# A three-part transformer kernel: gathers set between scatters, four places for normalised rows, and ScalarE in place of VectorE for attention's normalisation

## The chip, the cores and the metric

The kernel runs on 1 core of one Trainium2 chip. The metric is the device time of one execution in microseconds (us), as the median of several runs. The profile comes from one further execution of the same program. A measurement of this kernel tells about 0.5% from no change.

## The reference, cut to what matters

The input x has 4096 rows (2 sequences of 2048) of D = 256 floats. Three layers follow one another, each on a layer norm of x, each added to x:

```
x = x + 0.5 * ffn(layernorm(x))       # "FFN", first time
x = x + attention_and_moe(layernorm(x))
x = x + 0.5 * ffn(layernorm(x))       # "FFN", second time

ffn(h):   scores = sigmoid(h @ gate_w.T)              # 16 experts
          ids = top 512 rows of each expert           # "expert choice"
          eo = (silu(h[ids] @ gw.T + gb) * (h[ids] @ up.T + ub)) @ down.T + db
          out[ids] += eo * score;  out += shared_ffn(h)   # hidden 512

attention_and_moe(x):                                  # heads 16, width 16, chunks of 64
          y = rmsnorm(x) ; q, k = phi(rope(y @ Wq + bq)), phi(rope(y @ Wk + bk))
          v, g = y @ Wv + bv, sigmoid(y @ Wg + bg)
          S, Z run along the chunks of the sequence:   # linear attention
             S += k.T v ; Z += sum k ; o = g * (q S) / (q Z + 1e-6)
          x = x + o @ Wo + bo
          top 2 of 8 experts for each row, at most 1280 rows an expert:
          out[tok] += gate * (gelu(rmsnorm(x)[tok] @ W1 + b1) @ W2 + b2)
```

All products are wanted in float32. The kernel splits both factors of a large product in a high and a low part and takes three products of these (high by high, low by high, high by low).

## The kernel before, in words

Rows are kept in 32 tiles of 128. There are seven stretches in order of time, and the tensors' names tell them apart: f1s (front of the first FFN, `ffn_front`), f1e (its experts, `run_experts`), ma (`attention`), mr (routing), m (lists of the Mixture's rows), me (the Mixture's experts, `run_experts` again), f2s and f2e (second FFN). Each stretch is a block: every engine has its own queue of instructions there, written out in the order in which they are issued, with semaphores between the engines, and the next block begins when all engines are through.

**The front of the FFN.** Eight groups of four tiles. For each, VectorE takes means and variances, GpSimd (`root`) makes `rstd` and `shift`, ScalarE's `norm(g)` writes the normalised rows into `h[:, g % 2]`, a buffer with two places; TensorE's `turn(g)` transposes them, ScalarE casts the high part and `store(g)` sends the rows to DRAM (`h_rows`), where the gathers will read them. `norm(g)` therefore waits for the store of group g - 2 (`h_out`) and for its transposes (`turn_done`). Then come the products of the shared FFN in `STEPS` = 32 steps with their down products two steps behind, and between them the search for each expert's top 512 rows, whose lists are made by one-hot products: `slots(half, part)` is 32 products of 64 columns on TensorE, `place_ids(half)` 16 small operations of VectorE that turn the result into row numbers. `slots(1, 0)` and `slots(1, 1)` stand behind the last down product and `place_ids(1)` behind the last `add_shared`, which adds the shared FFN's output to x in `out`, another buffer with two places, which SyncE's queue (SP) stores.

**First rows.** At the end of a front and of the lists, `gather_first` on GpSimd fetches the first expert's rows: one indirect DMA for each tile of 128 rows (4 tiles for the FFN, 10 for the Mixture), and the block ends when they have been issued. `ids.shape[2]` is that number of tiles.

**The experts.** `run_experts` does E experts (16 for the FFN, called gated, with NT = 4 tiles; 8 for the Mixture, with NT = 10). The Mixture's hidden layer is 8 slices of 128 by C = 3 groups of up to 4 tiles, so S = 24 stages for an expert. In stage st TensorE makes the input product `into(e, st)` and the down product of two stages before, `down(e, st - 2)`; between them ScalarE takes the gelu (L1036) and VectorE splits it in a high and a low part. The rows of expert e + 1 are transposed in stages 13, 15, 17, 19 and 21 (`ITEM_AT`), two tiles each time, out of `rows`, a buffer with NT places. The output leaves PSUM by ScalarE (`read_sums`) and VectorE (`add_bias`, which counts `out_done`), and GpSimd scatters it tile by tile, adding in DRAM. `read_sums` of expert e + 1's last stages waits for `landed`, which GpSimd counts when the scatters of expert e - 1 are through.

GpSimd's queue in the experts is: the gathers of expert 1; then for each expert e, `gather_after(e + 1)`, which waits until the rows of expert e + 1 have been transposed and then issues all NT gathers of expert e + 2 in one go (L928), and then the NT scatters of expert e (L949), each behind its `out_done`. The gathers of expert e + 2 and the scatters of expert e so stand at the end of expert e and in the first stages of expert e + 1.

**Attention.** 32 tiles, two sequences by turns. `pipelined` gives each engine a list of steps with lags: in round r the engine does each step of its list for tile r - lag, in the order of the list. Ten rounds fill the pipeline, 22 run in a loop (11 times two), ten drain it. The steps that matter here are `stat` (VectorE, lag 0, last in its list: L1459 and L1461), `root` (GpSimd, lag 0, last, five operations), `norm` (VectorE, lag 1: two operations, L1466 and L1469, the layer norm into `x2_all` and the row scaled once more into `a`), TensorE's transposes of `a`, `split_at` (ScalarE, lag 2, first in its list, high part, L1405) and `split_low` (VectorE, lag 2, L1474). VectorE's list is:

```
pipelined(dve, T, [(10, add_out), (4, add_bias), (2, split_low), (6, state0), (7, state1), (5, feature),
                   (1, norm), (8, divide), (0, stat)])
```

and ScalarE's is `split_at` (2), `exp_rot` (5), `half_tanh` (4), `copy_qt` (6), `values` (5), `copy_ot` (9), `sum_squares` (10). SP loads tile r + 2's row of `x_all` (L1255) once `a` of a tile is done.

## Time and profile before

| | |
|---|---|
| runs | 2588.79, 2579.51, 2581.09 us; median 2581.09 |
| profiled execution | 2590.76 us, of which the span of the trace is 2589.0; mean granted TensorE clock 0.927 |
| busy, TensorE (PE) | 2288.6 us, 88% of the span |
| busy, VectorE (DVE) | 1764.9 us, 68% |
| busy, GpSimd (POOL) | 912.0 us, 35% |
| busy, ScalarE (ACT) | 846.1 us, 33% |

The stretches of the span, in us: front of the first FFN to about 229, its experts to 800, attention 820 to 1112, routing to 1162, lists to 1234, the Mixture's experts to 1777, front of the second FFN 1784 to 2011, its experts to 2583. In the profile PE is TensorE's matmuls and PEld its weight loads, which overlap; L12 is line 12 of the kernel before; a DMA share is the mean busy share of 16 DMA engines; the clock is the share of full speed (2.4 GHz) that the throttle granted. The idle time in brackets behind an instruction is that of its engine just ahead of it, with the event that came last before it ended.

### The profile page before, as it was taken

What the parts mean: (1) busy time and instruction counts of PE and PEld (TensorE: products, weight loads), DVE (VectorE), ACT (ScalarE), POOL (GpSimd) and SP (SyncE); (2) the same over time, 40 slices, a digit from 0 to 9 for tenths busy, and PEclk for the clock granted to TensorE, in tenths of its full rate; (3) what the DMA queues carried; (4) which work ended last, traced back from release to release, by engine and by line L of the source; (5) the groups of instructions that cost most, each with busy time, mean ns of one, the idle gap of its engine ahead of it and who ended that gap; (6) DMA issues with size and microseconds to landing.
All of it is one profiled execution on the core that took longest, in us unless ns stands there. A gap on an engine that the chain in (4) does not pass through costs nothing. (4 is left out here: it accounts for less than half of the span.)

```text
span 2589.0 us, 38567 instructions
## 1 busy us (share of the span) xinstructions
PE 2288.6 (88%) x13308; PEld 1974.0 (76%) x13308; DVE 1764.9 (68%) x3725; ACT 846.1 (33%) x1542; POOL 912.0 (35%) x965
## 2 busy tenths in 40 slices
PE   6998999999994888873799999993899899999997
PEld 5787888888883666661688888892778788888886
DVE  4785777777773999854465656553576777777775
ACT  5221333333331333310233333332321333333332
POOL 4201333333323877621144444424320233333332
PEclk9998999999997898955899999996999899999998
DMA  5003444444432000031243344325102344444442
GB/s 166 25 25 111 110 127 136 135 121 131 130 95 57 25 28 29 28 97 43 66 81 75 77 76 80 77 29 149 46 25 66 108 123 136 136 122 129 130 126 45
DMA packets 154183, 227.99 MB, mean 88 GB/s; under 512 B 33312, under 2 KB 104736, under 8 KB 153888
## 3 DMA queue, kind: packets, MB, share of 16 engines
q1 hardware_dynamic: 103184, 157.82, 19.5%
q0 software_dynamic: 39936, 55.93, 12.2%
q10 hardware_dynamic: 10896, 12.07, 1.4%
q8 instruction: 99, 1.62, 0.2%
q14 instruction: 68, 0.56, 0.1%
HBM read 171.36 MB, written 54.39 MB: 87 GB/s over the span
## 5 line engine op out<-in xcount | busy, mean ns | idle before, releaser
L1036 ACT ACTIVATE me_act_f<-me_in,me_bias 128x512 f32<-128x512 f32 (+1 forms) x192 | 118.6, 620 | 324.3 <-PE me_in L125 276.6
L123 PE MATMUL f1e_in<-f1e_xt_hi,f1e_w_hi 128*128 128x512 f32 x512 | 203.5, 398 | 2.4 <-DVE f1e_xt_lo L1096 2.4
L123 PE MATMUL f2e_in<-f2e_xt_hi,f2e_w_hi 128*128 128x512 f32 x512 | 203.4, 397 | 2.4 <-DVE f2e_xt_lo L1096 2.4
L125 PE MATMUL f2e_in<-f2e_xt_hi,f2e_w_lo 128*128 128x512 f32 x512 | 202.8, 396 | 0.0
L125 PE MATMUL f1e_in<-f1e_xt_hi,f1e_w_lo 128*128 128x512 f32 x512 | 202.7, 396 | 0.0
L124 PE MATMUL f1e_in<-f1e_xt_lo,f1e_w_hi 128*128 128x512 f32 x512 | 202.3, 395 | 0.0
L124 PE MATMUL f2e_in<-f2e_xt_lo,f2e_w_hi 128*128 128x512 f32 x512 | 202.2, 395 | 0.0
L1036 ACT ACTIVATE f1e_silu<-f1e_in,f1e_bias 128x512 f32<-128x512 f32 x128 | 88.2, 689 | 340.5 <-PE f1e_in L125 290.2
L1036 ACT ACTIVATE f2e_silu<-f2e_in,f2e_bias 128x512 f32<-128x512 f32 x128 | 88.2, 689 | 340.3 <-PE f2e_in L125 290.2
L1125 DVE CAST me_act_hi<-me_act_f 128x512 fp32r<-128x512 f32 (+1 forms) x192 | 74.6, 389 | 178.1 <-ACT me_act_f L1036 156.0
L123 PE MATMUL me_down<-me_w_hi,me_act_hi 128*128 128x256 f32 x640 | 184.2, 288 | 0.3 <-issue 0.2
L124 PE MATMUL me_down<-me_w_lo,me_act_hi 128*128 128x256 f32 x640 | 181.1, 283 | 0.3 <-issue 0.3
L125 PE MATMUL me_down<-me_w_hi,me_act_lo 128*128 128x256 f32 x640 | 180.5, 282 | 0.3 <-issue 0.3
L123 PE MATMUL me_in<-me_xt_hi,me_w_hi 128*128 128x512 f32 (+1 forms) x384 | 141.1, 368 | 35.8 <-DVE me_act_lo L1126 20.9
L1122 DVE SCALAR_TENSOR_TENSOR f1e_act_f<-f1e_in,f1e_bias,f1e_silu 128x512 f32<-128x512 f32 x128 | 96.0, 750 | 112.5 <-ACT f1e_silu L1036 85.5
L1122 DVE SCALAR_TENSOR_TENSOR f2e_act_f<-f2e_in,f2e_bias,f2e_silu 128x512 f32<-128x512 f32 x128 | 96.0, 750 | 112.4 <-ACT f2e_silu L1036 84.1
L949 POOL DMA_INDIRECT out<-f2e_out,f2e_sid x64 | 107.6, 1682 | 167.1 <-DVE f2e_out L1139 152.4
L949 POOL DMA_INDIRECT after_ffn<-f1e_out,f1e_sid x64 | 107.3, 1677 | 166.8 <-DVE f1e_out L1139 152.2
L949 POOL DMA_INDIRECT after_moe<-me_out,me_sid x80 | 131.5, 1643 | 92.7 <-DVE me_out L1139 70.0
L123 PE MATMUL f1e_down<-f1e_w_hi,f1e_act_hi 128*128 128x256 f32 x512 | 147.3, 288 | 0.0
L123 PE MATMUL f2e_down<-f2e_w_hi,f2e_act_hi 128*128 128x256 f32 x512 | 147.2, 288 | 0.0
L125 PE MATMUL f2e_down<-f2e_w_hi,f2e_act_lo 128*128 128x256 f32 x512 | 144.3, 282 | 0.0
(429 smaller groups left out, 7053.7 us busy)
## 6 DMA issues: line engine op xcount, KB each, us to landing
f_raw<-in_ffn_w SPq DMA_DIRECT2D x256, 384.0 KB
m_raw<-in_moe_w SPq DMA_DIRECT2D x64, 256.0 KB
f1s_x_all<-in_x SPq DMA_DIRECT2D x8, 512.0 KB, 8.5
f_h<-f1s_h ACTq DMA_DIRECT2D x8, 512.0 KB, 3.0
after_ffn<-f1s_out SPq DMA_DIRECT2D x8, 512.0 KB, 3.1
ma_x_all<-after_ffn SPq DMA_DIRECT2D x32, 128.0 KB
after_moe<-ma_x_all SPq DMA_DIRECT2D x32, 128.0 KB
m_h<-mr_h SPq DMA_DIRECT2D x16, 256.0 KB, 2.2
```

What stands on the lines that cost most here:

```text
L123: pe.matmul(out, lh, rh, start=first, stop=False, skip_group_check=True)
L124: pe.matmul(out, lh, rl, start=False, stop=False, skip_group_check=True)
L125: return pe.matmul(out, ll, rh, start=False, stop=last, skip_group_check=True)
L949: pool.indirect_dma_start(out=acc, out_offset=bass.IndirectOffsetOnAxis(ap=sid[:, j:j + 1], axis=0), in_=out[:, b, j, :], in_offset=None, ...
L1036: act.activation(dst[:, st % 2, 0:n], ps_in[st % 2][0][:, 0:n], func, bias=bias[:, b, f:f + 1]).then_inc(silu_done, 1)
L1122: own.step(dve.scalar_tensor_tensor(act_n, ps_in[st % 2][1][:, 0:n], bias[:, b, F_T + f:F_T + f + 1], silu[:, st % 2, 0:n], ALU.add, ALU.m ...
L1125: own.step(dve.tensor_copy(hi_n, act_n))
```

## The change

Three sets of edits.

First, in the experts. `gather_first` fetches `FIRST_TILES` = 4 tiles; where NT is larger (the Mixture), the other six are gathered at the start of `run_experts`. For the Mixture, each of expert 1's ten gathers waits for one further down product, and those of expert e + 2 are issued one behind each scatter of expert e. The FFN keeps its order. Second, in the front. Normalised rows have `H_RING` = 4 places (the two of `h` and, while it isn't used, the two of `out`), so that `norm(g)` waits for group g - 4; the first two `add_shared` wait for the stores and transposes of those places. `slots(1, 0)` and `slots(1, 1)` move ahead of the last two down products, `place_ids(0)` goes from the start of step `STEPS` to its end, and `place_ids(1)` moves ahead of the last `add_shared`. Third, in attention. ScalarE takes `norm` over, first in its list, as two activations with a scale and a shift; GpSimd's `root` has three operations instead of five (one power over two columns, one shift) and VectorE's `stat` also waits for `a_done` ahead of L1461.

```diff
...
@@ -48,7 +48,7 @@
...
-RAW_RING = 4
+RAW_RING, FIRST_TILES = 4, 4
...
@@ -156,7 +156,7 @@
 
     pool.tensor_copy(first.gid[:], ids[:, 0, :]).then_inc(first.gid_done, 1)
     wait_apart(pool, first.gid_done, 1)
-    for j in range(ids.shape[2]):
+    for j in range(FIRST_TILES):
         pool.indirect_dma_start(out=first.rows[:, j, :], out_offset=None, in_=h_rows,
                                 in_offset=bass.IndirectOffsetOnAxis(ap=first.gid[:, j:j + 1], axis=0)
                                 ).then_inc(first.rows_in[j // 2], 16)
...
+    H_RING = 4
...
+        h_ring = [h[:, 0], h[:, 1], out[:, 0], out[:, 1]]
...
@@ -331,7 +333,7 @@
                 for k in range(K):
                     for t in range(GT):
                         ins = pe.transpose(turned[g % 2][:, k * GC + t * P:k * GC + (t + 1) * P],
-                                           h[:, g % 2, t, k * P:(k + 1) * P], ident[:])
+                                           h_ring[g % H_RING][:, t, k * P:(k + 1) * P], ident[:])
                 ins.then_inc(turn_done, 1)
...
+            last = {STEPS: lambda: slots(1, 0), STEPS + 1: lambda: slots(1, 1)}
             extra = {LISTS + 1: [lambda: offset(0)], LISTS + 2: [lambda: offset(1)], LISTS + 3: [turn_positions],
                      LISTS + 9: [lambda: slots(0, 0)], LISTS + 10: [lambda: slots(0, 1)]}
             for g in range(G + 1):
@@ -438,10 +441,10 @@
                     into(n)
                 for one in extra.get(n, ()):
                     one()
+                if n in last:
+                    last[n]()
                 if n >= LAG:
                     down(n - LAG)
-            slots(1, 0)
-            slots(1, 1)
...
             def norm(g):
-                u = g % 2
+                u = g % H_RING
                 act.wait_ge(x_in_s[g], 16)
                 act.wait_ge(rstd_done, g + 1)
-                if g >= 2:
-                    act.wait_ge(h_out[u], 16 * (g // 2))
-                    act.wait_ge(turn_done, g - 1)
+                if g >= H_RING:
+                    act.wait_ge(h_out[u], 16 * (g // H_RING))
+                    act.wait_ge(turn_done, g - H_RING + 1)
                 for t in range(GT):
-                    ins = act.activation(h[:, u, t], x_all[:, g * GT + t], ACT.Identity, bias=shift[:, g, t:t + 1],
+                    ins = act.activation(h_ring[u][:, t], x_all[:, g * GT + t], ACT.Identity, bias=shift[:, g, t:t + 1],
                                          scale=rstd[:, g, t:t + 1])
                 ins.then_inc(h_done, 1)
...
             def store(g):
                 act.wait_ge(h_done, g + 1)
-                act.dma_start(rows_of(h_rows, g), h[:, g % 2]).then_inc(h_out[g % 2], 16)
+                act.dma_start(rows_of(h_rows, g), h_ring[g % H_RING]).then_inc(h_out[g % H_RING], 16)
...
         def _(dve):
@@ -575,6 +578,9 @@
                 dve.wait_ge(down_done, (g + 1) * F_T)
                 if g >= 2:
                     dve.wait_ge(out_stored[g % 2], 16 * (g // 2))
+                else:
+                    dve.wait_ge(h_out[2 + g], 16 * (G // H_RING))
+                    dve.wait_ge(turn_done, G)
                 for t in range(0, GT, 2):
                     ins = dve.scalar_tensor_tensor(out[:, g % 2, t:t + 2], ps_down[:, t:t + 2, :], 0.5,
                                                    x_all[:, g * GT + t:g * GT + t + 2, :], ALU.mult, ALU.add)
...
-            lists = {STEPS: lambda: place_ids(0), LISTS: choose, LISTS + 1: add_ties, LISTS + 2: place, LISTS + 3: split_positions}
+            lists = {LISTS: choose, LISTS + 1: add_ties, LISTS + 2: place, LISTS + 3: split_positions}
...
@@ -678,9 +684,12 @@
                     activate(n)
                 if n - 1 >= LISTS and n - 1 < STEPS:
                     activation_low(n - 1)
+                if n == STEPS:
+                    place_ids(0)
+                if n + 1 == STEPS + LAG:
+                    place_ids(1)
                 if ends_group(n + 1):
                     add_shared((n + 1 - LAG) // F_T - 1)
-            place_ids(1)
             dve.wait_ge(ids_done, 2)
...
-            def gather(e):
-                own.step(pool.tensor_copy(gid[:], gather_ids[:, ds(e, 1), :].rearrange("p e j -> p (e j)")), apart=True)
-                for j in range(NT):
-                    pool.indirect_dma_start(out=rows[:, j, :], out_offset=None, in_=h_rows,
-                                            in_offset=bass.IndirectOffsetOnAxis(ap=gid[:, j:j + 1], axis=0)
-                                            ).then_inc(rows_in[j // 2], 16)
-
-            def gather_after(e):
+            def take_ids(dst, ids, e):
+                own.step(pool.tensor_copy(dst[:], ids[:, ds(e, 1), :].rearrange("p e j -> p (e j)")), apart=True)
+
+            def gather_tile(j):
+                pool.indirect_dma_start(out=rows[:, j, :], out_offset=None, in_=h_rows,
+                                        in_offset=bass.IndirectOffsetOnAxis(ap=gid[:, j:j + 1], axis=0)
+                                        ).then_inc(rows_in[j // 2], 16)
+
+            def rows_free(e):
 
                 pool.wait_ge(gates_set, e + 1)
                 pool.wait_ge(turned, e * NI + NI)
                 for i in range(NI):
                     wait_apart(pool, rows_in[i], e * 32 + 32)
-                gather(e + 1)
-
-            gather_after(0)
+
+            def scatter_tile(e, b, j):
+                pool.wait_ge(out_done, (e + OUT0) * NT + j + 1)
+                pool.indirect_dma_start(out=acc, out_offset=bass.IndirectOffsetOnAxis(ap=sid[:, j:j + 1], axis=0),
+                                        in_=out[:, b, j, :], in_offset=None, compute_op=ALU.add
+                                        ).then_inc(scattered, 16)
+
+            if NT > FIRST_TILES:
+                take_ids(gid, gather_ids, 0)
+                for j in range(FIRST_TILES, NT):
+                    gather_tile(j)
+            rows_free(0)
+            take_ids(gid, gather_ids, 1)
+            for j in range(NT):
+                if not gated:
+                    pool.wait_ge(down_done, DOWN0 + j + 2)
+                gather_tile(j)
 
             def one(e, b, left):
+
                 if left > 1:
-                    gather_after(e + 1)
-
-                own.step(pool.tensor_copy(sid[:], scatter_ids[:, ds(e, 1), :].rearrange("p e j -> p (e j)")))
+                    rows_free(e + 1)
+                    take_ids(gid, gather_ids, e + 2)
+                    if gated:
+                        for j in range(NT):
+                            gather_tile(j)
+                take_ids(sid, scatter_ids, e)
                 for j in range(NT):
-                    pool.wait_ge(out_done, (e + OUT0) * NT + j + 1)
-                    pool.indirect_dma_start(out=acc, out_offset=bass.IndirectOffsetOnAxis(ap=sid[:, j:j + 1], axis=0),
-                                            in_=out[:, b, j, :], in_offset=None, compute_op=ALU.add
-                                            ).then_inc(scattered, 16)
+                    scatter_tile(e, b, j)
+                    if left > 1 and not gated:
+                        gather_tile(j)
                 pool.wait_ge(scattered, e * (16 * NT) + 16 * NT)
                 pool.nop().then_inc(landed, 1)
 
...
@@ -1272,16 +1299,11 @@
                 h = q * 2 + u
                 wait_apart(pool, a_done, h + 1)
...
-                var = mv[:, u, 1:2]
-                pool.tensor_scalar(rs[:, u, 0:1], var, EPS, None, ALU.add).then_inc(own_var, 1)
+                pool.tensor_scalar(mv[:, u, 2:3], mv[:, u, 1:2], EPS, None, ALU.add).then_inc(own_var, 1)
                 pool.wait_ge(own_var, h + 1)
-                pool.tensor_tensor(rs[:, u, 1:2], rs[:, u, 0:1], neg_half[:], ALU.pow).then_inc(own_inv, 1)
-                pool.wait_ge(own_inv, h + 1)
-                pool.tensor_tensor(rs[:, u, 2:3], rs[:, u, 1:2], rs[:, u, 1:2], ALU.mult).then_inc(own_sq, 1)
-                pool.wait_ge(own_sq, h + 1)
-                pool.tensor_tensor(rs[:, u, 2:3], rs[:, u, 2:3], var, ALU.mult).then_inc(own_ratio, 1)
-                pool.wait_ge(own_ratio, h + 1)
-                pool.tensor_tensor(rs[:, u, 3:4], rs[:, u, 2:3], neg_half[:], ALU.pow).then_inc(rs_done, 1)
+                pool.tensor_tensor(rs[:, u], mv[:, u, 1:3], neg_half[:], ALU.pow).then_inc(own_inv, 1)
+                wait_apart(pool, own_inv, h + 1)
+                pool.tensor_scalar(shift[:, u], rs[:, u], mv[:, u, 0:1], -1.0, ALU.mult, ALU.mult).then_inc(rs_done, 1)
...
+            def norm(q, u):
+                h = q * 2 + u
+                act.wait_ge(rs_done, h + 1)
+                act.wait_ge(a_turned, h + 1)
+                act.activation(row(x2_all, q, u), row(x_all, q, u), ACT.Identity, bias=shift[:, u, 1:2], scale=rs[:, u, 1:2])
+                act.activation(a[:, u], row(x_all, q, u), ACT.Identity, bias=shift[:, u, 0:1], scale=rs[:, u, 0:1]
+                               ).then_inc(a_done, 1)
+
             def split_at(q, u):
                 h = q * 2 + u
-                act.wait_ge(a_turned, h + 1)
+                act.wait_ge(a_turned, h + 3)
                 act.wait_ge(proj_done, h + 1)
...
-            pipelined(act, T, [(2, split_at), (5, exp_rot), (4, half_tanh), (6, copy_qt), (5, values), (9, copy_ot),
+            pipelined(act, T, [(1, norm), (2, split_at), (5, exp_rot), (4, half_tanh), (6, copy_qt), (5, values), (9, copy_ot),
                                (10, sum_squares)])
...
-            for sem, free in ((a_done, 2), (at_done, 1), (proj_done, 2), (proj_read, 1), (rot_done, 2), (er_done, 2), (s1_done, 2),
...
-                dve.bn_aggr(mv[:, u], stats[:, u]).then_inc(stat_done, 1)
-
-            def norm(q, u):
-                h = q * 2 + u
-                dve.wait_ge(rs_done, h + 1)
-                dve.tensor_scalar(row(x2_all, q, u), row(x_all, q, u), mv[:, u, 0:1], rs[:, u, 1:2], ALU.subtract,
-                                  ALU.mult).then_inc(own_xt, 1)
-                dve.wait_ge(own_xt, h + 1)
-                dve.tensor_scalar(a[:, u], row(x2_all, q, u), rs[:, u, 3:4], None, ALU.mult).then_inc(a_done, 1)
+                wait_apart(dve, a_done, h + 1)
+                dve.bn_aggr(mv[:, u, 0:2], stats[:, u]).then_inc(stat_done, 1)
...
             pipelined(dve, T, [(10, add_out), (4, add_bias), (2, split_low), (6, state0), (7, state1), (5, feature),
-                               (1, norm), (8, divide), (0, stat)])
+                               (8, divide), (0, stat)])
```

## Rows read from the trace of the kernel before

**Rows 1.** Busy time by stretch: attention's loop, Mixture's experts, second FFN's experts.
```profile
core 0: us, PE busy (x) PEld busy (x) DVE busy (x) ACT busy (x) POOL busy (x), PEclk, DMA share, GB/s
876.00:1060.00 184.00, 159.23 (x793) 119.32 (x791) 170.80 (x377) 66.88 (x204) 135.37 (x210) 0.88 0.09 30
...
1330.00:1760.00 430.00, 400.50 (x2728) 368.43 (x2726) 255.71 (x510) 150.58 (x282) 169.40 (x132) 0.98 0.36 68
2030.00:2589.00 559.00, 542.47 (x3144) 475.21 (x3142) 407.14 (x638) 198.49 (x310) 177.44 (x150) 0.99 0.43 117
```

**Rows 2.** Loads of attention's loop: duration ns, first and last start.
```profile
L1255 SPq MOVE ma_x_all<-after_ffn x22: 29/29/29, 876.6 to 1061.5; - x22
```

**Rows 3.** Busy time, stages 0 to 6 of Mixture's experts 1, 2, 5, 6, 7.
```profile
1313.74:1330.85 17.11, 14.37 (x97) 12.99 (x97) 10.90 (x24) 6.83 (x16) 14.08 (x12) 1.00 0.80 123
1374.95:1397.01 22.06, 16.32 (x97) 14.31 (x97) 11.38 (x24) 6.93 (x15) 18.03 (x15) 0.92 0.54 116
...
1570.81:1589.37 18.56, 14.53 (x97) 12.98 (x97) 10.95 (x24) 6.75 (x15) 15.15 (x13) 1.00 0.76 123
1633.47:1654.69 21.22, 16.08 (x97) 14.29 (x97) 10.95 (x24) 6.80 (x16) 17.19 (x15) 0.92 0.58 116
1698.84:1714.34 15.50, 14.06 (x97) 12.89 (x97) 11.22 (x24) 6.84 (x15) 11.88 (x8) 1.00 0.45 52
```

**Rows 4.** Busy time, stages 6 to 24 of Mixture's expert 1.
```profile
1330.85:1374.95 44.10, 44.10 (x311) 40.83 (x310) 27.74 (x53) 15.61 (x29) 14.53 (x11) 1.00 0.34 65
```

**Rows 5.** Timeline, expert 2's stage 3: start, us, instruction, idle before it.
```profile
1383.13 0.39 PE L125 MATMUL me_in<-me_xt_hi,me_w_lo 128*128 128x512 f32 x1
...
1389.76 0.69 ACT L1036 ACTIVATE me_act_f<-me_in,me_bias 128x512 f32<-128x512 f32 x1 [8.28 <-DMA f1s_x_all<-in_x]
```

**Rows 6.** Timeline of GpSimd there: first and fifth gather, one scatter.
```profile
1372.17 1.27 POOL L928 DMA_INDIRECT m_rows<-m_h,me_gid  x1 [0.83 <-POOL me_gid L926]
...
1377.61 1.13 POOL L928 DMA_INDIRECT m_rows<-m_h,me_gid  x1 [0.30 <-issue]
...
1385.97 1.63 POOL L949 DMA_INDIRECT after_moe<-me_out,me_sid  x1 [0.28 <-POOL me_sid L946]
```

**Rows 7.** Timeline, lists' end and experts' start: gathers 4 and 10, first cast, third turn.
```profile
1222.11 0.95 POOL L160 DMA_INDIRECT m_rows<-m_h,m_gid  x1 [0.30 <-issue]
...
1229.61 0.94 POOL L160 DMA_INDIRECT m_rows<-m_h,m_gid  x1 [0.30 <-issue]
...
1234.60 2.18 ACT L1025 CAST me_w_hi<-m_raw 128x512 fp32r<-128x512 f32 x4 [68.52 <-DVEq L1084]
...
1242.94 1.06 PE L965 MATMUL me_turn<-m_ident,m_rows 128*128 128x128 f32 x4
```

**Rows 8.** Timeline, front of the first FFN: ScalarE's norm of group 2.
```profile
21.25 2.07 ACT L459 ACTIVATE f1s_h<-f1s_x_all,f1s_shift,f1s_rstd 128x256 f32<-128x256 f32 x4 [5.98 <-DMA f_h<-f1s_h]
```

**Rows 9.** Timeline, end of the second FFN's front.
```profile
1999.23 0.38 PE L123 MATMUL f2s_down<-f2s_w_hi,f2s_act_hi 128*128 128x256 f32 x1 [1.76 <-DVE f2s_act_lo L571]
2000.74 7.27 PE L420 MATMUL f2s_wide<-f2s_x_all,f2s_hot 128*128 128x64 f16 x64
2000.94 1.29 DVE L579 SCALAR_TENSOR_TENSOR f2s_out<-f2s_down,f2s_x_all 128x512 f32<-128x512 f32 x2 [1.76 <-PE f2s_down L125]
2008.05 2.80 DVE L648 TENSOR_SCALAR f_ids<-f2s_wide 32x8 uint32<-32x8 f32 x16 [5.82 <-PE f2s_wide L420]
```

**Rows 10.** DMA issues of the page: KB each, median us from issue to landing.
```profile
after_ffn<-f1s_out SPq DMA_DIRECT2D x8, 512.0 KB, 3.1
```

**Rows 11.** Timeline of one round of attention's loop.
```profile
967.91 0.63 ACT L1405 ACTIVATE ma_at_hi<-ma_ps_a,ma_scale 128x128 fp32r<-128x128 f32 x2 [4.36 <-PE ma_ps_a L1325]
...
969.37 0.18 DVE L1461 BATCH_NORM_AGGREGATE ma_mv<-ma_stats 128x2 f32<-128x6 f32 x1
...
971.87 0.60 DVE L1474 SCALAR_TENSOR_TENSOR ma_at_lo<-ma_ps_a,ma_scale,ma_at_hi 128x128 fp32r<-128x128 f32 x2
...
973.70 0.81 DVE L1466 TENSOR_SCALAR m_x_all<-ma_x_all,ma_mv,ma_rs  x1
...
975.78 0.16 DVE L1514 TENSOR_SCALAR ma_den<-ma_ps_num 128x16 f32<-128x16 f32 x1
```

## Prediction before the run

> **What bounds the kernel now.** I read the page first (its busy shares, its forty slices, its DMA groups), then tables of busy time for each stretch, one attention round and one boundary between experts instruction by instruction, and GpSimd's own instructions. No engine bounds the whole. In the FFN experts TensorE is the bound, 542.47 of 559 us busy, and in the Mixture experts nearly so, 400.50 of 430 [rows 1]; the reader should see that the two differ although the same function makes both. In attention VectorE has the most to do, 170.80 of 184 us, with TensorE second at 159.23 and a granted clock of only 0.88 [rows 1]. 22 loads of the attention loop start from 876.6 to 1061.5, so a round takes 184.9/21 = 8.80 us [rows 2].
>
> The Mixture's missing time lies in one place. Stages 0 to 6 of experts 1 to 7 take 17.11, 22.06, 20.50, 20.98, 18.56, 21.22 and 15.50 us (five of these seven stand in [rows 3]); stages 6 to 24 take 44.10 with TensorE busy for 44.10 [rows 4]. The first six have the ten gathers of the next expert's rows in them, the last has none, and their excesses over 15.50 are 1.61 + 6.56 + 5.00 + 5.48 + 3.06 + 5.72 = 27.4 us. At 1383.13 TensorE has issued the last input product of a stage, 0.39 us long, but ScalarE's gelu, which waits for it, starts at 1389.76, after 8.28 idle [rows 5]: completions arrive late, and nothing that the trace names is late ahead of them (the view puts the wait down to a long finished load, so its name means nothing). This begins at about the fifth gather, 1377.61 after a first at 1372.17 [rows 6]. The FFN issues four in a row and shows none of it [rows 1].
>
> **The change, step by step**, against the profiled execution: 2590.76 us, span 2589.0. That is 9.7 above the median of the runs, 2581.09, so I take 9.7 off at the end.
>
> *Mixture's gathers between scatters: -27.4.* Nothing is removed; a pair is one scatter (1.63) and one gather (0.95 to 1.27), each with 0.3 of issue [rows 6], about 3.2 us, ten pairs 32 us. They stand where the ten scatters already run, and the rows are first needed at stage 13, so no turn comes late: scatters follow the last three down steps, the boundary stages take 15.5 and seven more 44.1/18 x 7 = 17, and gather 2 is done at about 6 us, gather 10 at 32 (the last pair is turned at stage 21, at about 52). Behind a waiting gather on GpSimd stands the next scatter, and behind ten scatters the count that lets the next output be written at stage 21; ten gathers of 1.25 put between them are the same ten gathers that stand ahead of them now, so the last scatter ends no later: nothing. Bounds: 0 if the lateness belongs to gathers wherever they stand, -27.4 if it belongs to the burst. I take the burst, since the first four of one are harmless here and in the FFN.
>
> *Expert 1's gathers, one for each down step from stage 0 on: -1* (0 to -2, bounded by expert 1's excess of 1.61).
>
> *Four tiles first: -7.5.* The fourth gather of the Mixture's lists starts at 1222.11 and the tenth at 1229.61, and the expert phase begins at 1234.60, when they are through [rows 7]: 7.5 us of GpSimd alone, 1.25 a gather. Six gathers move into the phase's start, with a copy of the list (0.7). TensorE turns tiles 4 and 5 at 1242.94 now, 8.3 us behind the phase's start [rows 7]; the fifth gather will be issued within 2 us of the start and the tenth within 9, and the turns of tiles 4 to 9 stand one behind another from there. Bounds: -7.5, and -4 if the last turn waits.
>
> *Fronts: 2 x (-4.5 + 1.1) = -6.8.* ScalarE's norm of group 2 waits 5.98 us for the store of group 0 [rows 8]. With four places it waits for nothing: group 4 needs that store by about 3 us later than it lands. The group's new limit is ScalarE's norm, 2.07 [rows 8], and two casts, about 3.7 together, of which some 1.5 is not covered by the 5.98: -4.5 (bounds -3 to -6). Behind norm stand the casts and the stores on ScalarE's queue, which all move up. At the end, TensorE idles 1.76 ahead of the last down product (1999.23), then runs 64 one-hot products, 7.27 from 2000.74, and VectorE the ids, 2.80 from 2008.05 to 2010.85 [rows 9]. After: the first 32 products fill the 1.76, the other half and the down products end about 2006.3, VectorE has done the ids at about 2007.5, adds the last group (1.3, [rows 9]), and its store takes 3.1 [rows 10]: about 2011.9, +1.1. What hid the last store before (the products and ids) is gone, which is why 3.1 comes back. Bounds -1.5 to +1.5. SP loads the experts' first weights behind these products, a little earlier. The places of group 2 and 3 are the output's buffers: the add of groups 0 and 1 waits for stores long landed.
>
> *Attention: -27.* VectorE loses two operations, 973.70 to 975.78 = 2.08 of a round [rows 11], to ScalarE, busy for 66.88 of 184 [rows 1]. VectorE's round, 170.80/20.9 = 8.17 busy, falls to 6.1 busy, 6.73 with its present gaps. What is late next: VectorE takes its statistics (ends t = 969.55), GpSimd now needs three operations instead of five (0.2 + 0.57 + 0.2 and what lies between, about 1.3), ScalarE normalises (2 x 0.55, like the 128x256 ones of [rows 8], 2.07 for four) and scales the high part (0.63, [rows 11]), so VectorE's low part can start at t + 3.2 instead of t + 2.3 (971.87, [rows 11]). With the rest of its round behind it this makes 7.5. TensorE is close: 159.23/20.9 = 7.6 a round at the clock of 0.88, 6.7 were it at full speed throughout, and 0.5 of gaps: 7.2 to 8.1. I take 7.8, bounds 7.48 and 8.3: 22 x (8.80 - 7.8) = 22, and the 20 rounds of filling and draining, where some of the same chain shows, about 5. The added wait of the statistics for ScalarE's norm of two rounds before is met long ahead. ScalarE's norm waits at the head of its queue for GpSimd, and behind it stand the high part, exp, tanh and the copies that TensorE waits for.
>
> A rule of the Trainium skill says otherwise of ScalarE's price ("VectorE: DVE Perf Modes", the section on the TRN2 errata): an SBUF to SBUF instruction costs 224 cycles plus its elements at 1.2 GHz, an estimate of 0.40 us for 256. The four in 2.07 us of [rows 8] are 0.52 each. By the page the sum would be 0.25 a round better, 5 us in all; the trace decides.
>
> **Sum:** -27.4 - 1 - 7.5 - 6.8 - 27 = -69.7, so 2521.1 for a profiled execution like this one, and about 2511 for the median.
>
> **Rivals.**
> (A) *The gathers cost the same wherever they stand*, chance 0.2, with B 0.08 more. Nothing in the trace shows why completions come late, and DMA is only 0.54 busy at the worst boundary [rows 3]; scatters with gathers between could be just as long a burst of indirect transfers. For it: expert 1 to 2's boundary loses only 1.6 with the same burst, so the link is loose. Against: the excess is never there with ten scatters alone (15.50, [rows 3]). Time: 2511 + 27.4 + 1 = 2539. The skill's page "SBUF — State Buffer" ("Who interferes with whom") holds that a DMA never contends with a compute engine and that TensorE and ScalarE wait on nobody; by that rule the gathers are innocent and spacing them gives nothing, so it speaks for this rival, and the rows of late completions speak against it.
> (B) *TensorE bounds attention*: its clock stays at 0.88 and its round at 8.3, so half the gain is left: 22 x 0.5 + 3 = 14, time 2524. Chance 0.15. For it: 7.6 busy a round against a round of 7.8 leaves no room; against: a fuller TensorE may be granted a higher clock, as in [rows 4], 1.00 where it never idles.
> (C) *Slower than before: ScalarE's norm, first in its queue, closes a loop.* Norm waits for GpSimd, GpSimd for the statistics, the statistics come last in VectorE's round, behind the divide, which waits for TensorE's numerators, which wait for exp and the copies behind norm in ScalarE's queue. If that chain had to be gone through once a round, TensorE's and ScalarE's work would stand one behind the other: 7.6 + 66.88/20.9 + 1.1 for the norm = 11.9 [rows 1], 22 x (11.9 - 8.8) = +68, and 2581.1 - 42.7 + 68 = 2606. From a round of 10.7 on it outweighs the 42.7 of the other parts. Against it: exp, values and numerators work on tiles of earlier rounds, so the chain spans two rounds, 6.0 each. Chance 0.04.
> (D) *The change of the fronts and lists only shifts waits*: each 2 to 4 us short, inside the range.
>
> **How the numbers follow.** Forecast's own case 0.5, with 2494 to 2524 as its range (attention's bounds and the fronts', -11 and +13, and what a run differs by). A 0.2, B 0.15, both 0.08, C 0.04, and 0.03 for a loss that I don't see. The range, 2494 to 2553, takes in A, B and both together and leaves out C. The measurement can tell 0.5%, 13 us: faster means below 2568, slower above 2594. Everything but C and the last 0.03 is below 2568, save some of that with A and B and fronts that also fail: faster 0.89, same 0.05, slower 0.06.
>
> **What would show each step.** Stages 0 to 6 of experts 2 to 6 at 15.5 to 16.5 each, and gelu right behind its product (A: still 18 to 22). The expert phase of the Mixture starting 5 us or so behind the fourth gather. ScalarE's norm of group 2 without a wait, the products ahead of the last down products, and the front ended by a store. Attention's loads 7.8 apart, VectorE busy below 0.82 of a round (B: 8.3, with TensorE above 0.9 busy; C: above 10.7). I am wrong above 2553 if spacing brings nothing and attention gains less than half.

## The result, and the profile after

The changed kernel took 2522.39 us in the median (2519.79 to 2524.34), the kernel before 2582.86 (2579.51 to 2588.79) beside it: ratio 0.9763, 95% interval 0.9741 to 0.9785. That is 60 us, where 70 were forecast for the profiled execution and the median alike. The two profiled spans differ by 71.0 (2589.0 and 2518.0). By stretch, a front read from ScalarE's first norm and every other stretch as named:

| stretch | before | after | difference | forecast |
|---|---|---|---|---|
| front, first FFN (to the experts' first cast) | 221.3 | 212.8 | -8.5 | -3.4 |
| experts, first FFN | 576.8 | 575.8 | -1.0 | 0 |
| attention (first load to the routing's start) | 305.9 | 289.1 | -16.8 | -27 |
| routing and lists | 121.5 | 112.6 | -8.9 | -7.5 |
| Mixture's experts, first gelu to last | 508.8 | 480.6 | -28.2 | -28.4 |
| front, second FFN | 220.3 | 213.4 | -6.9 | -3.4 |
| experts, second FFN | 576.6 | 576.0 | -0.6 | 0 |

The sum of the profiled spans came out right by luck in part: two errors stood against each other, attention 10 too much and the fronts 8.6 too little. Busy time by stretch of the changed kernel, for attention's loop and for stages 0 to 6 of the Mixture's experts 2, 5 and 6 ([rows 1, 3] before):

```profile
core 0: us, PE busy (x) PEld busy (x) DVE busy (x) ACT busy (x) POOL busy (x), PEclk, DMA share, GB/s
869.90:1036.60 166.70, 148.63 (x800) 105.67 (x799) 144.54 (x337) 88.21 (x254) 124.45 (x168) 1.00 0.10 33
1336.96:1352.54 15.58, 14.22 (x97) 12.97 (x97) 11.08 (x24) 6.84 (x15) 12.14 (x9) 1.00 0.55 107
1515.86:1531.36 15.50, 14.18 (x97) 12.94 (x97) 11.08 (x24) 6.83 (x15) 12.07 (x9) 1.00 0.54 106
1575.46:1591.04 15.58, 14.22 (x97) 12.97 (x97) 11.08 (x24) 6.84 (x15) 12.15 (x9) 1.00 0.57 106
```

The boundaries of 22.06, 18.56 and 21.22 us are now 15.5, with the same 97 products. Attention's loop is shorter, VectorE's share fell from 0.93 to 0.87, and TensorE's clock rose from 0.88 to 1.00. The loads of attention's loop (tile view, duration in ns, first and last start; [rows 2] before):

```profile
L1282 SPq MOVE ma_x_all<-after_ffn x22: 29/29/29, 870.4 to 1037.0; - x22
```

166.6/21 = 7.93 us a round, after 8.80. One round on the timeline, from the end of VectorE's statistics to its low part ([rows 11] before):

```profile
954.19 0.18 DVE L1492 BATCH_NORM_AGGREGATE ma_mv<-ma_stats 128x2 f32<-128x6 f32 x1 [0.17 <-DVE ma_stats L1489]
...
954.54 0.22 POOL L1302 TENSOR_SCALAR ma_mv<-ma_mv 128x1 f32<-128x1 f32 x1 [0.73 <-DVE ma_mv L1492]
...
954.85 0.72 POOL L1304 TENSOR_TENSOR ma_rs<-ma_mv,ma_neg_half 128x2 f32<-128x2 f32 x1
...
955.75 0.27 POOL L1306 TENSOR_SCALAR ma_shift<-ma_rs,ma_mv 128x2 f32<-128x2 f32 x1 [0.18 <-POOL ma_rs L1304]
...
956.15 0.60 ACT L1426 ACTIVATE m_x_all<-ma_x_all,ma_shift,ma_rs  x1 [3.79 <-POOL ma_shift L1306]
...
956.66 0.59 ACT L1427 ACTIVATE ma_a<-ma_x_all,ma_shift,ma_rs 128x256 f32 x1
...
957.15 0.60 ACT L1435 ACTIVATE ma_at_hi<-ma_ps_a,ma_scale 128x128 fp32r<-128x128 f32 x2
...
957.79 0.61 DVE L1497 SCALAR_TENSOR_TENSOR ma_at_lo<-ma_ps_a,ma_scale,ma_at_hi 128x128 fp32r<-128x128 f32 x2 [0.50 <-ACT ma_at_hi L1435]
```

Read it downwards: statistics end at t = 954.37, the shift at t + 1.65, norm begins at t + 1.78 after ScalarE has idled 3.79 for it, and VectorE's low part begins at t + 3.42 after 0.50 idle. The chain is the one forecast, 0.2 longer than forecast: GpSimd's part takes 1.65 where 1.3 was expected, with a power over two columns of 0.72. The round closes over it. In the mean of the loop, VectorE needs 4.51 us from the start of one low part to the end of the next statistics, without a wait for another engine, and 3.42 pass from there to the next low part: 7.93.

VectorE didn't get all of its time back. It lost two operations of 2.1 us, but its busy time a round fell from 8.17 to 144.54/21 = 6.88, where 6.1 was forecast. One of its operations that stayed, before and after, each with GpSimd's addition beside it:

```profile
971.27 0.68 DVE L1486 TENSOR_TENSOR ma_rot_a<-ma_qk,ma_rope 128x512 f32<-128x512 f32 x1
...
971.72 0.83 POOL L1307 TENSOR_TENSOR ma_x_all<-ma_x_all,m_x_all  x1
```
```profile
956.01 0.73 POOL L1329 TENSOR_TENSOR ma_x_all<-ma_x_all,m_x_all  x1
...
956.10 1.19 DVE L1509 TENSOR_TENSOR ma_rot_a<-ma_qk,ma_rope 128x512 f32<-128x512 f32 x1
```

Where VectorE's operation starts first it takes 0.68; where it starts 0.09 behind GpSimd's it takes 1.19, and it does so in every round (1.11 to 1.21). The step behind the reciprocal (`ma_div`) went from 0.73 to 0.88. That the overlap with GpSimd is the cause is an inference from these rows; no run removes it.

In the rounds that fill the pipeline, VectorE's wait for the high part is much longer than the 0.50 above:

```profile
832.27 0.27 POOL L1306 TENSOR_SCALAR ma_shift<-ma_rs,ma_mv 128x2 f32<-128x2 f32 x1 [0.18 <-POOL ma_rs L1304]
...
832.57 0.61 ACT L1426 ACTIVATE m_x_all<-ma_x_all,ma_shift,ma_rs 128x256 f32<-128x256 f32 x1 [4.68 <-POOL ma_shift L1306]
...
833.57 0.60 ACT L1435 ACTIVATE ma_at_hi<-ma_ps_a,ma_scale 128x128 fp32r<-128x128 f32 x2
...
834.21 0.61 DVE L1497 SCALAR_TENSOR_TENSOR ma_at_lo<-ma_ps_a,ma_scale,ma_at_hi 128x128 fp32r<-128x128 f32 x2 [2.70 <-ACT ma_at_hi L1435]
```

VectorE idles 2.70 us for the high part of tile r - 2. Its transposes were issued at 829.36, over 4 us earlier; the high part stands in ScalarE's queue behind norm of tile r - 1, which waits for GpSimd.

ScalarE on the timeline of the first front ([rows 8] before):

```profile
15.01 2.08 ACT L462 ACTIVATE f1s_out<-f1s_x_all,f1s_shift,f1s_rstd 128x256 f32<-128x256 f32 x4
...
17.88 2.09 ACT L462 ACTIVATE f1s_out<-f1s_x_all,f1s_shift,f1s_rstd 128x256 f32<-128x256 f32 x4
```

and the end of the second front ([rows 9] before):

```profile
1929.80 3.59 PE L422 MATMUL f2s_wide<-f2s_x_all,f2s_hot 128*128 128x64 f16 x31
...
1933.43 2.80 DVE L654 TENSOR_SCALAR f_ids<-f2s_wide 32x8 uint32<-32x8 f32 x16 [5.15 <-PE f2s_wide L422]
...
1936.26 1.29 DVE L585 SCALAR_TENSOR_TENSOR f2s_out<-f2s_down,f2s_x_all 128x512 f32<-128x512 f32 x2
1937.58 0.40 SPq L278 DMA_DIRECT2D out<-f2s_out  x1
...
1942.00 3.04 ACT L1052 CAST f2e_w_hi<-f_raw 128x768 fp32r<-128x768 f32 x4 [17.15 <-DVEq L1111]
```

Norm of group 2 starts at 15.01 instead of 21.25, with no wait, and group 3 follows at 17.88. At the end the products stand ahead of the last down products and the ids are done at 1936.23. The last thing ahead of the next block is now the store, issued at 1937.58; the block begins 4.4 us later, at 1942.00. At the Mixture's start the experts' first cast follows the fourth gather by 3.9 us, where about 5 were forecast; before, it followed the tenth by 4.99 ([rows 7]):

```profile
1195.35 0.95 POOL L160 DMA_INDIRECT m_rows<-m_h,m_gid  x1 [0.30 <-issue]
...
1199.26 2.18 ACT L1052 CAST me_w_hi<-m_raw 128x512 fp32r<-128x512 f32 x4 [59.76 <-DVEq L1111]
```

### The profile page after: what moved, and what is told of

Same layout as the page of the kernel before. It is cut to its first block and busy times, and to the rows that moved or that the text cites. A ratio compares the mean times of both kernels' runs of the same rounds, so it can differ in the third digit from the quotient of the medians.

```text
span 2518.0 us, 38628 instructions
## 1 busy us (share of the span) xinstructions
PE 2257.9 (90%) x13308; PEld 1945.4 (77%) x13308; DVE 1729.2 (69%) x3661; ACT 876.4 (35%) x1606; POOL 888.2 (35%) x902
## 5 line engine op out<-in xcount | busy, mean ns | idle before, releaser
L951 POOL DMA_INDIRECT after_ffn<-f1e_out,f1e_sid x64 | 102.1, 1596 | 159.3 <-DVE f1e_out L1166 144.7
L951 POOL DMA_INDIRECT out<-f2e_out,f2e_sid x64 | 102.1, 1595 | 159.4 <-DVE f2e_out L1166 144.8
```

The costliest lines, as they stand in the source:

```text
L951: pool.indirect_dma_start(out=acc, out_offset=bass.IndirectOffsetOnAxis(ap=sid[:, j:j + 1], axis=0), in_=out[:, b, j, :], in_offset=None, ...
```

## The experiments

The pair above and three more sets of four kernels ran, each set on one chip and with the kernel before beside it; the three later sets ran on three different chips. Its median was 2582.9, 2578.0, 2562.5 and 2571.2 us in these four sets: this spread of 20 us in one and the same kernel turned out to be part of the answer. The ratios of the parts are to the kernel before of the same set. "Excess" below is the sum of stages 0 to 6 of experts 1 to 6 less 6 x 15.50, from the trace of each kernel.

**1. The gathers spaced, and nothing else** (the kernel before with `FIRST_TILES` = 10 and the new order of gathers and scatters, expert 1's ten gathers spaced too).

```diff
                 if left > 1:
-                    gather_after(e + 1)
...
+                    rows_free(e + 1)
+                    take_ids(gid, gather_ids, e + 2)
...
+                    scatter_tile(e, b, j)
+                    if left > 1 and not gated:
+                        gather_tile(j)
```

> Before with the Mixture's gathers spaced and nothing else: all ten first tiles are still fetched ahead of the experts, fronts and attention are as before. Theory (the burst of ten gathers makes completions late): stages 0 to 6 of experts 2 to 6 at 15.5 to 16 us each, 26 to 28 us less than in the profile of before, and a ratio of about 0.989 to 0.991. The pair of medians after/before moved by 60, 10 less than the two profiles, so the burst may cost less in most executions than in the profiled one: then the ratio is nearer to 0.993. Rival (gathers cost the same wherever they stand): stages 0 to 6 stay at 18 to 22, ratio 0.998 to 1.001.

Measured: 2558.73 against 2577.98, ratio 0.9926 (0.9908 to 0.9944), 19 us. Excess 0.1; stages 0 to 6 of expert 2 by busy time:

```profile
1371.16:1386.66 15.50, 14.17 (x97) 12.94 (x97) 11.08 (x24) 6.83 (x15) 12.07 (x9) 1.00 0.58 106
```

The excess goes with nothing else changed, so rival A is wrong. The median gains 19 and not 27, and the runs lie closer together than those of the kernel before: 2558.05 to 2560.76, against 2574.16 to 2586.18.

**2. Four places for rows, and nothing else.**

```diff
-                u = g % 2
+                u = g % H_RING
...
-                if g >= 2:
+                if g >= H_RING:
```

> Before with four places for normalised rows and nothing else; the one-hot products stay at the end. Theory, from the two profiles (last score product 6.7 us earlier in the first front, 5.0 in the second, and some 2 more by the third stage of products): fronts 8.5 and 7.5 us shorter, ratio about 0.994. Rival (my forecast's size, one wait of 5.98 partly covered): 4.5 us each, ratio 0.9965. If much of the saving came from the moved products, less than 0.998 is not reached.

Measured: ratio 0.9961 (0.9946 to 0.9976), 10 us. Fronts 213.7 and 215.0 us.

**3. The one-hot products moved, and nothing else.**

```diff
+                if n in last:
+                    last[n]()
                 if n >= LAG:
                     down(n - LAG)
-            slots(1, 0)
-            slots(1, 1)
...
+                if n == STEPS:
+                    place_ids(0)
+                if n + 1 == STEPS + LAG:
+                    place_ids(1)
```

> Before with the second half of the one-hot products among the last steps, the ids ahead of the last add, and nothing else. Theory, from the two profiles (the experts follow the last step 0.6 us later than before): each front +0.6 us, ratio 1.000 to 1.001. Rival (the products fill the idle 1.8 us and shorten the end): -1 to -2 each, ratio 0.9985 to 0.9995.

Measured: ratio 1.0006 (0.9988 to 1.0023). Fronts 222.8 and 218.6. No gain, and no loss beyond 6 us. Over all traces, the four with neither edit have fronts of 220.2 and 219.5 in the mean, the eight with both 215.0 and 215.9: 5.2 + 3.6 = 8.8 us for the pair, where the first two profiles alone said 15.4. A front of the same code varied by up to 4 us.

**4. ScalarE's norm in attention, and nothing else.**

```diff
-            pipelined(act, T, [(2, split_at), (5, exp_rot), (4, half_tanh), (6, copy_qt), (5, values), (9, copy_ot),
+            pipelined(act, T, [(1, norm), (2, split_at), (5, exp_rot), (4, half_tanh), (6, copy_qt), (5, values), (9, copy_ot),
...
```

> Before with ScalarE's normalisation in attention and nothing else. Theory (it is independent of the other parts): rounds of 7.93 us, 19 less in the loop, the filling of the pipeline 3 longer, 17 us in all, ratio 0.9935, granted clock 1.00 in the loop. Rival (the clock of 1.00 came from elsewhere, such as the other parts' timing): the clock stays at 0.88 and the round comes to 8.3 or more, ratio 0.996.

Measured: ratio 0.9966 (0.9953 to 0.9979), 9 us, but attention itself went from 305.9 to 287.8 and the round to 7.93 with a clock of 1.00. Attention alone does what it does in the whole. The missing 9 us are not in its stretch: the excess of this kernel is 20.3, and expert 4 the longest boundary of any trace:

```profile
1482.30:1505.60 23.30, 17.51 (x97) 15.20 (x97) 11.25 (x24) 6.84 (x16) 18.95 (x16) 0.85 0.70 111
```

The parts measured alone sum to less than the whole (19 + 10 + 9, with 9 for the lists 47, against 60): kernels with the burst in them carry its noise, and a ratio of one of them to the kernel before compares two amounts of it. Taking each kernel's excess off its profiled execution shows this. Three kernels that differ from the kernel before in nothing that gains (before, before again in experiment 9, products moved) come to 2563.4, 2562.6 and 2562.8 us. Against their mean of 2563 the rest is:

| | profiled execution less excess | gain |
|---|---|---|
| spaced | 2558.4 | 5 |
| four places | 2554.2 | 9 |
| attention | 2544.6 | 18 |
| the changed kernel | 2519.6 | 43 |

The three gains and 9 for the lists make 41, against 43: without the excess the parts add up, within what a front varies by.

**5. The burst again, in the changed kernel.**

```diff
-                    if gated:
-                        for j in range(NT):
-                            gather_tile(j)
+                    for j in range(NT):
+                        gather_tile(j)
                 take_ids(sid, scatter_ids, e)
                 for j in range(NT):
                     scatter_tile(e, b, j)
-                    if left > 1 and not gated:
-                        gather_tile(j)
```

> After with one thing undone: the ten gathers of expert e + 2 in one go ahead of expert e's scatters (four first tiles and expert 1's spacing kept). Theory (the burst costs what the first experiment gave, 19 us in the median): 2522 + 19 = 2541 to 2545, ratio to before 0.984 to 0.986, stages 0 to 6 of experts 1 to 6 from 17 to 23 us. The three parts measured alone (19, 10 and 8) sum to 37, with some 9 for the first tiles 46, and the whole gave 60; if the burst costs more in a kernel whose other parts are changed, this one is 28 us or more above after, ratio 0.988 or more.

Measured: 2523.22 us, no slower than the changed kernel, beside a kernel before of 2562.49: ratio 0.9848 (0.9831 to 0.9866). Excess 0.4. The price of 19 us that was expected isn't there. Busy time of expert 2's and 6's stages 0 to 6:

```profile
1337.32:1352.83 15.51, 14.05 (x97) 12.87 (x97) 11.25 (x24) 6.83 (x15) 12.17 (x11) 1.00 0.52 128
1576.00:1591.58 15.58, 14.14 (x97) 12.93 (x97) 11.25 (x24) 6.84 (x15) 12.22 (x11) 1.00 0.51 129
```

GpSimd's timeline there, the first and the fifth gather:

```profile
1334.54 1.27 POOL L938 DMA_INDIRECT m_rows<-m_h,me_gid  x1 [0.83 <-POOL me_gid L935]
...
1339.98 1.13 POOL L938 DMA_INDIRECT m_rows<-m_h,me_gid  x1 [0.30 <-issue]
```

The fifth gather stands 5.44 us behind the first, exactly as in [rows 6], and 2.66 us into the first stage, as there (1377.61 - 1374.95 = 2.66): the same burst at the same place, with no late completion.

**6 to 8. Other orders of the ten gathers**, in the same set: five in one go and five in pairs; all ten in one go behind the scatters; ten ahead of the scatters, each for one more down product.

```diff
+                    for j in range(NT if gated else 5):          # 6
+                        gather_tile(j)
...
+                    if left > 1 and not gated and j >= 5:
+                        gather_tile(j)
```
```diff
+                if left > 1 and not gated:                       # 7, behind the loop of scatters
+                    for j in range(NT):
+                        gather_tile(j)
```
```diff
+                    for j in range(NT):                          # 8
+                        if not gated:
+                            pool.wait_ge(down_done, DOWN0 + e * S + 22 + j)
+                        gather_tile(j)
...
```

> After with five gathers in one go and the last five one behind each of the last five scatters. Theory of my prediction (completions are late from about the fifth gather of a burst on): stages 0 to 6 of experts 1 to 6 at 15.5 to 16, at most one late completion in each. Rival (every back-to-back pair of gathers beside the boundary's work costs its share): half of the excess, 1 to 3 us a boundary.

> After with the ten gathers in one go, but behind the ten scatters, so that they run at stages 8 to 13 of the expert and not over its first stages. If the burst makes completions late wherever it stands: late completions of 2 us and more there, and stages 6 to 24 longer than 44.1 by 2 to 6 us each, as stages 0 to 6 were before. Rival (it is the boundary's own work, the output's reads and the bias and weight loads, that the burst collides with): stages 0 to 6 at 15.5 and 6 to 24 at 44.1. The rows are turned from stage 13 on, about 32 us after the expert's start, and the gathers end at about 33, so a wait of a few us at stage 13 may show in either case, at TensorE's turn and not at gelu.

> After with the ten gathers ahead of the scatters as before, but each waiting for one further down product, so 2.45 us apart and with no scatter between. Theory (spacing is what counts): stages 0 to 6 at 15.5 to 15.7 and 44.1 for the rest, as in after; the scatters start later, at stage 8, and end at about 40 us, ahead of stage 21, which waits for them. Rival (it is the mixture with scatters that helps): excess of 1 us or more a boundary.

Measured, one execution each: 2523.22, 2526.67 and 2523.34, excess 0.3, 0.9 and 0.2. In a set where the burst itself cost nothing they tell nothing apart. Whether the fifth gather is a limit, or where a burst may stand, was not settled.

**9 and 10. The kernel before and the burst of experiment 5 once more**, both unchanged, on one chip.

> The kernel before, unchanged, profiled anew. In the second set of runs the kernel before took 2562 us, not 2578 to 2582 as in the others, and the burst of gathers cost nothing. If that is a property of the chip (or of where the program's memory lies) and not of the kernel, this profile and its median go together: at about 2578 its boundaries take 17 to 22 us, at about 2562 they take 15.5 to 15.7 with the gathers at the same times in the stage. If the boundaries take 17 to 22 at 2562, the 16 us came from elsewhere.

> The burst restored in the changed kernel, once more, beside a profile of the kernel before from the same chip. If the burst's price belongs to the chip: excess of stages 0 to 6 here as in that profile (both about 0, or both 14 to 28 us), ratio to before 0.985 in either case. If it belongs to the other parts of the change (the first tiles, or expert 1's spaced gathers): none here (480.7 us from the first gelu to the last), even where that profile has 14 us or more; ratio 0.978.

Measured: the kernel before 2566.16 in this execution (2571.21 in the median of the set), excess 3.6; the other 2529.43 in the median (2523.61 to 2536.47), excess 2.2, nearly all of it at expert 3; ratio 0.9843 (0.9823 to 0.9863). Two boundaries of the kernel before, experts 2 and 5:

```profile
1373.37:1388.87 15.50, 14.08 (x97) 12.89 (x97) 11.21 (x24) 6.84 (x16) 12.38 (x12) 1.00 0.53 131
1553.68:1570.66 16.98, 14.28 (x97) 12.92 (x97) 11.10 (x24) 6.83 (x15) 13.82 (x12) 1.00 0.76 122
```

The first was 22.06 in [rows 3], of the same program. So the price of the burst isn't fixed by the program: it differs from one execution to another, and by the set. Whether the chip or something else makes the sets differ isn't told apart, since the three later sets each had a chip of their own:

| set, its median of the kernel before | kernels with the burst: excess | spaced: excess |
|---|---|---|
| 2582.9 | before 27.4 | after 0.2 |
| 2578.0 | four places 14.8, products moved 14.4, attention 20.3 | spaced 0.1 |
| 2562.5 | burst again 0.4 | 0.2 |
| 2571.2 | before 3.6, burst again 2.2 | 0.2 (twice) |

**11. ScalarE's high part ahead of its norm.**

```diff
-            pipelined(act, T, [(1, norm), (2, split_at), (5, exp_rot), (4, half_tanh), (6, copy_qt), (5, values), (9, copy_ot),
+            pipelined(act, T, [(2, split_at), (1, norm), (5, exp_rot), (4, half_tanh), (6, copy_qt), (5, values), (9, copy_ot),
```

> After with ScalarE's scaling of the high part (lag 2) ahead of its norm (lag 1). Theory (in the filling rounds VectorE's low part waits 1.8 to 2.7 us for a high part that stands behind norm, and 0.3 to 0.5 in the loop): the filling goes back from 73 to 70 us, the loop's round from 7.93 to 7.5 to 7.8, 5 to 10 us in all. Rival (TensorE sets the round: 7.08 us busy of 7.93 at full clock, and norm comes 0.6 us later to its transposes): the filling 3 shorter, the round 7.9 or 0.1 longer, 0 to 3 us in all.

Measured: 2517.31 us (2514.45 to 2518.08), ratio to the kernel before 0.9789 (0.9775 to 0.9802). Attention takes 282.2 us, 6.9 less than in the changed kernel: the filling 69.0 instead of 72.9, ten rounds as long as before the change (69.5), the loop 164.7 instead of 166.7, so 7.84 a round, the draining 1.0 less.

**12. One more activation in norm.** It writes 128x256 to a spare buffer that nothing reads.

```diff
...
+                act.activation(spare[:], row(x_all, q, u), ACT.Identity, bias=shift[:, u, 1:2], scale=rs[:, u, 1:2])
                 act.activation(a[:, u], row(x_all, q, u), ACT.Identity, bias=shift[:, u, 0:1], scale=rs[:, u, 0:1]
```

> After with one more activation of 128x256 (its output is not used) between ScalarE's two of norm, 0.5 to 0.6 us longer. If the chain from the statistics over GpSimd and norm to the low part sets the loop's round: 7.93 + 0.5 = 8.4 to 8.5, the loop 10 to 12 us longer. If TensorE sets it and ScalarE has slack: 7.9 to 8.1, at most 3 us.

Measured: 2545.77, rounds of 8.73 us, attention 309.3. The loop is 16.7 us longer, 0.80 a round for one activation, more than the 0.5 that was expected. What VectorE's low part waited for in these kernels (tile view; us of idle time ahead of it, times), in the changed kernel:

```profile
its engine sat idle before it (us, times) until:
  ACT ma_at_hi L1435: 29.4, 31
```

in experiment 11:

```profile
  ACT ma_at_hi L1435: 6.4, 3
```

and in experiment 12:

```profile
  ACT ma_at_hi L1437: 45.3, 31
```

29.4 us in 31 rounds, gone but for 6.4 when the high part goes first, and 45.3 with a longer norm. The two legs of the round, in the mean of each loop:

| | low part to the end of the statistics (VectorE) | from there to the next low part | round |
|---|---|---|---|
| changed kernel | 4.51 | 3.42, of it 0.39 idle ahead of the low part | 7.93 |
| 12, longer norm | 4.82 | 3.91, of it 0.88 idle | 8.73 |
| 11, high part first | 4.89 | 2.95, nothing idle | 7.84 |

The longer norm adds 0.49 to the second leg, what one more activation takes in ScalarE's queue (the three start 0.50 apart). The other 0.31 is VectorE's: its feature step (`ma_phi`), now beside another of GpSimd's operations, takes 1.50 instead of 0.74, and the division 0.43 instead of 0.88. So the chain from the statistics over GpSimd and norm to the low part is part of the changed kernel's round, and VectorE's own list the other part. With the high part first the chain is out of it, and yet the round is only 0.1 shorter: VectorE is then busy for 150.80 of 164.70 us, 7.18 a round, the other 0.66 are short gaps in its own list, and it waits for no other engine. Its `ma_rot_a` takes 1.16 there and `ma_phi` 1.12, against 0.68 and 0.70 in the kernel before. That VectorE sets this round is read from the trace; no run tests it.

## Why the prediction was right, and where it was wrong

The median lay in the range, within the forecast's own case, though 11 us above its 2511. Point by point:

- **Gathers between scatters, -27.4.** That the order is what matters is shown: with the same work and only the order changed, the excess is 0.1 in a set in which three kernels with the burst have 14 to 20 (experiment 1). Why the burst makes completions late isn't. The size was that of one profiled execution. It is 27 in that, some 19 in the median of the second set, and 0.4 and 2 to 4 in the profiled executions of the two other sets. The failing step is the one in which 9.7 us were taken off at the end as if they had nothing to do with the terms: the profiled execution of before lay above its median, and the likeliest reason is the very excess of which the change removes all: less its excess it comes to 2563.4, and the one of experiment 9 to 2562.6 (and the runs of a spaced kernel spread over 3 to 5 us, those of a kernel with the burst over 5 to 22 in the sets that show the excess, the kernel before over 2 in the set that doesn't). With 19 for this term, taken from the median, the forecast would have been about 2520. The medians' own excess wasn't profiled. The Trainium skill's rule ("SBUF — State Buffer", "Who interferes with whom") that DMA never contends with a compute engine would have had the order of the gathers cost nothing: two sets nearly agree, and the ratio of 0.9926 in a third speaks against it.
- **Rival A** (gathers cost the same wherever they stand) is wrong by the same experiment, in the sets where the burst costs anything.
- **Expert 1's gathers, -1.** Stages 0 to 6 of expert 0, where they stand, take 24.3 us in the mean of the nine traces with that edit and 25.1 in that of the five without it: -0.7, though the ranges overlap (24.0 to 25.3 and 24.5 to 25.4). The prediction bounded the term by expert 1's excess of 1.61, which is already in the 27.4.
- **The fifth gather as the point where it begins** is neither shown nor refuted: the kernel with a burst of ten had no late completion in the set that was to test it.
- **Four tiles first, -7.5.** Right: 8.9 less in routing and lists, about the six gathers of 1.25 and 1.1 less between the last gather and the experts' first cast. From that cast to the first gelu it is 9.91 before and after, and the third turn stands 8.34 behind it in both, so the later gathers cost nothing.
- **Fronts, -6.8.** The mechanism is right (norm of group 2 has no wait). The profiles said -15.4, but a front of one code varies by 4 us, and the mean over twelve traces is -8.8. So rival D (the fronts and lists only shift waits) is wrong. The +1.1 for the end, which becomes the store's, agrees with a ratio of 1.0006 for that edit alone, though this can't be told from none. ScalarE's price for attention's norm was right too: its two activations take 0.60 and 0.59 and start 0.51 apart. The 0.40 of the Trainium skill ("VectorE: DVE Perf Modes", the section on the TRN2 errata) is shorter than these rows, though a plain copy of the same size in the same loop (`ma_v`, L1450) takes 0.41.
- **Attention, -27, of it 22 in the loop and 5 in filling and draining.** The loop gave 18.3 over 21 intervals, a round of 7.93 where 7.8 was taken. The step that was mis-sized there is VectorE's relief: its round was to fall to 6.1 us busy and measured 6.88, since operations that stayed got longer beside GpSimd's. The term that failed is the ramp: forecast -5, measured 3.4 more in filling and 2.0 less in draining. "Some of the same chain shows" was taken as a gain. The chain that replaces VectorE's work is a loss where VectorE isn't full: it idles 2.70 us at 834.21 for a high part that stands behind norm. The prediction named what is queued behind norm and didn't price it where the pipeline fills; experiment 11 shows that it is this order, since the filling goes back to 69.0.
- **Rival B** (TensorE at 0.88 bounds at 8.3): its clock was 1.00, its busy time a round fell from 7.6 to 148.63/21 = 7.1, and the round is 7.93, the sum of the two legs above, in which TensorE isn't waited for. Wrong.
- **Rival C** (norm at the head closes a loop) is right that a loop closes over norm and wrong in which: not over exp, the copies and the numerators, but over the high part, the low part and VectorE's own list, 7.93 and not 11.9. The place at the head costs 0.1 a round and 4 us of filling.

## What to carry to other kernels

A step handed to an idle engine brings its wait with it: put it behind those steps of that engine which need nothing new (here 6.9 us, by exchanging two entries of a list), and look for its price where the pipeline fills, not only in the steady round. Don't book the whole length of the operations taken away: measure the busy time of the relieved engine again, since what stays can get longer when it shifts against another engine's work. When a profiled execution is slower than its median, ask first whether the stall that you are about to price is what makes it slower, and price it by the median. Parts measured alone against a kernel that carries a variable stall each inherit its noise; take the stall out first and measure the rest on top.

## What the runs showed of the hardware that was not expected

One program's boundary of six stages took 22.06 us in one execution and 15.50 in another, with GpSimd's gathers at the same times and 97 matmuls in both; the late completions of TensorE during back-to-back indirect gathers came in strength in two of four sets (excess 14 to 27 us), weakly in the last (2 to 4) and not in the third (0.4). What makes them late stays open. A VectorE operation with two inputs of 128x512 took 0.68 us where it started ahead of GpSimd's addition and 1.19 where it started 0.09 behind it. And attention's loop was granted a clock of 0.88 with TensorE busy for 87% of it, and 1.00 with 89%; with one more activation a round the loop is nearly as long as before (183.30 us), TensorE busy for 151.01 of it, 82%, and the clock still 0.99:

```profile
874.80:1058.10 183.30, 151.01 (x808) 107.42 (x807) 150.64 (x336) 98.26 (x275) 121.29 (x169) 0.99 0.10 30
```
